# Building the attention's search mask on TensorE: scores made a second time, the masked gap added to them, and the engines' slots redone

## The reference, cut to what matters

```python
scores = jnp.einsum('bthd,bghd->bhtg', Q, K) / np.sqrt(DH)
scores = jnp.where(vision_mask[:, None, None, :], scores, -jnp.inf)
topv, topi = jax.lax.top_k(scores, K_TOP)          # K_TOP = 32
probs = jax.nn.softmax(topv, axis=-1)
attn = jnp.zeros_like(scores).at[bi, hi, ti, topi].set(probs)
attn_mean = attn.mean(axis=1)                      # over the 4 heads
c_t = jnp.einsum('btg,bgd->btd', attn_mean, V)
```

## Time and profile before

| | us |
|---|---|
| three runs, median (lowest, highest) | 1743.46 (1742.68, 1745.92) |
| the profiled execution's own time | 1737.76 |
| its span, first to last instruction | 1735.6 |
| mean granted TensorE clock in it | 0.959 |

### The profile page before, as it was taken

One profiled execution on the slowest core, in us unless ns is written; L12 is line 12 of the kernel. 1 busy time (PEld: TensorE's weight loads), 2 busy tenths in 40 slices (PEclk: granted clock), 3 DMA queues, 4 the chain that ended last, 5 costly groups with the idle time before them and its releaser, 6 DMA issues.

```text
span 1735.6 us, 22438 instructions
## 1 busy us (share of the span) xinstructions
PE 1535.6 (88%) x7358; PEld 1135.2 (65%) x7369; DVE 1350.4 (78%) x2168; ACT 1146.9 (66%) x2101; POOL 1195.9 (69%) x1341
## 2 busy tenths in 40 slices
PE   4878868898889898889998999899989998999996
PEld 2456546665656565667686767676767776767896
DVE  5798799988998898978888888888888995111321
ACT  2388875686678658765887588757876687134442
POOL 1388775858876786788678876897689858633422
PEclk9899889998998999899999999999999999999999
DMA  7210031002200210123322331333132211842431
GB/s 199 54 34 4 20 104 31 13 19 61 43 13 25 64 35 13 36 74 95 95 73 62 76 94 51 76 82 98 46 80 65 86 32 40 266 143 88 95 50 22
DMA packets 97223, 115.27 MB, mean 66 GB/s; under 512 B 17840, under 2 KB 74168, under 8 KB 96964
## 3 DMA queue, kind: packets, MB, share of 16 engines
q1 hardware_dynamic: 85348, 100.32, 19.9%
q0 software_dynamic: 11760, 13.52, 5.2%
HBM read 75.48 MB, written 19.58 MB: 55 GB/s over the span
## 4 chain that ended last, share of the span: by engine, by line
PE 31%; DVE 28%; POOL 16%; ACT 16%; issue 7%; DMA 2%; SPq 1%; POOLq 0%; DVEq 0%
DVE R L1460 9%; DVE ZB L1464 7%; POOL ZB L773 4%; PE PS L2191 4%; DVE ZB L1456 4%; ACT ZB L1049 3%; PE PS L2039 3%; PE PS L1770 3%; PE PS L2068 2%; DVE R L1452 2%; ACT R L1052 2%; ACT R L1055 2%; PE PS L1820 2%; POOL ZB L775 2%; PE PS L2027 2%
## 5 line engine op out<-in xcount | busy, mean ns | idle before, releaser
L1460 DVE MAX8 R<-ZB 128x8 f32<-128x1024 f32 x384 | 471.1, 1227 | 10.9
L1770 PE MATMUL PS<-R 128*128 128x256 f32 x1118 | 290.4, 394 | 26.0 <-ACT R L1052 14.6
L1464 DVE MATCH_REPLACE8 ZB<-R,ZB 128x1024 f32<-128x1024 f32 x256 | 309.5, 1209 | 0.0
L773 POOL TENSOR_TENSOR ZB<-ZB 128x1024 f32<-128x1024 f32 x96 | 231.7, 2414 | 68.4 <-ACT ZB L1049 68.2
L1052 ACT ACTIVATE R<-PS 128x512 f32<-128x512 f32 (+6 forms) x404 | 173.3, 467 | 143.2 <-PE PS L2039 47.3
L1770 PEld LDWEIGHTS PS<-R 128*128 128x128 f32 x1118 | 211.2, 198 | 72.7 <-ACT R L1052 24.2
L775 POOL TENSOR_TENSOR ZB<-ZB 128x1024 f32<-128x1024 f32 x96 | 226.6, 2360 | 7.5
L1452 DVE MAX8 R<-PS 128x8 f32<-128x1024 f32 x128 | 155.9, 1218 | 6.9 <-PE PS L1793 6.9
L1456 DVE MATCH_REPLACE8 ZB<-R,PS 128x1024 f32<-128x1024 f32 x128 | 155.5, 1215 | 0.0
L1049 ACT ACTIVATE ZB<-ZB,R 128x1024 f32<-128x1024 f32 x128 | 147.1, 1149 | 4.2
L1049 ACT ACTIVATE ZB<-PS,R 128x1024 f32<-128x1024 f32 x128 | 141.6, 1106 | 3.1 <-DVE R L1472 2.8
(11 more groups left out here) (256 smaller groups left out, 3150.1 us busy)
## 6 DMA issues: line engine op xcount, KB each, us to landing
ZR<-ZR SPq DMA_DIRECT2D x96, 128.0 KB
ZB<-in_L_ffn_rt_gate SPq DMA_DIRECT2D x21, 512.0 KB
ZB<-in_L_ffn_rt_up SPq DMA_DIRECT2D x21, 512.0 KB
ZB<-in_L_ffn_rt_down SPq DMA_DIRECT2D x21, 512.0 KB, 5.9
R<-in_x SPq DMA_DIRECT2D x16, 512.0 KB, 3.9
ZB<-in_ctx SPq DMA_DIRECT2D x8, 768.0 KB, 4.8
R<-xs_d SPq DMA_DIRECT2D x39, 128.5 KB, 2.1
out<-R SPq DMA_DIRECT2D x32, 128.0 KB, 3.7
```

What stands on the lines that cost most here:

```text
L773: pool.tensor_tensor(e, e, w, ALU.mult).then_inc(s.g_att, 1)
L1460: vec.max(ml[:, 8 * r:8 * r + 8], w).then_inc(s_tk[n % 2], 1)
L1464: vec.match_replace(w, ml[:, 8 * r:8 * r + 8], w, NEG).then_inc(s_tk[n % 2], 1)
L1770: pe.matmul(q_bank(*key)[:, 0:256], ident, warm, start=True, stop=True)
```

## The change

The mask no longer is an array that POOL multiplies with. Once the 32nd largest is known, ACT writes the gap as bf16 into `gap[n % 2]` (the first half of tk's words). PE then makes the scores a second time into the same banks and adds, by one more bf16 matmul per bank with a diagonal `steep` of -2^66, the gap times -2^66 (`cuts`, four matmuls a unit). ACT takes one exponential of the result, with -max*SCALE - log(sum) as its bias, so that e comes out masked and divided by the sum. POOL only adds: three additions for four heads (head 0 and 1 in one), none for the first. The second DVE operation of `limits` becomes a tensor_scalar with two operations in place of the reciprocal.

The waits follow: the scores of n+2 now wait for the exponential of n (a_att), which waits for the cut of n (p_cut), which waits for the gap (a_gap). The first replacement of n+2 waits for the cut of n instead of POOL's product. Transfers that refill qt and kt wait for the cuts.

`warm` is now R[:, 0:256], and keep_warm waits for the constants instead of tri. The loads of gout and bout share a semaphore with gin, bin and b2. All slot tables are new. The FILL tables sum to 413 matmuls over the kernel where they summed to 559.

```diff
-        warm = R[:, alloc.top:alloc.top + 256]
+        warm = R[:, 0:256]
...
+        gap = [w[:, 0:512].bitcast(BF16) for w in tk]
         ee = [alloc_b(1024), alloc_b(1024)]
+        steep = alloc_b(64).bitcast(BF16)
...
@@ sync
-                        on.wait_ge(s.p_sc, 16 * (b - 1) + 8)
+                        on.wait_ge(s.p_cut, 16 * (b - 1) + 8)
...
@@ gpsimd attention
-                    on.wait_ge(s.a_att, 5 * n + 5)
-                    if h == 0:
+                    on.wait_ge(s.a_att, n + 1)
+                    if h == 1:
                         if t:
                             on.wait_ge(*q_run("finish", t - 1, 1))
-                        pool.tensor_tensor(acc, e, w, ALU.mult).then_inc(s.g_att, 1)
+                        pool.tensor_tensor(acc, ee[0], ee[1], ALU.add).then_inc(s.g_att, 1)
                     else:
-                        pool.tensor_tensor(e, e, w, ALU.mult).then_inc(s.g_att, 1)
-                        on.wait_ge(s.g_att, 7 * t + 2 * h)
-                        pool.tensor_tensor(acc, acc, e, ALU.add).then_inc(s.g_att, 1)
+                        on.wait_ge(s.g_att, 3 * t + h - 1)
+                        pool.tensor_tensor(acc, acc, ee[n % 2], ALU.add).then_inc(s.g_att, 1)
...
@@ scalar
+            def limits():
+                for n in range(16 * B):
+                    ml, q = mx[n % 3], sm[n % 3]
+                    yield tile_at(n) + ACT_GAP[n % 16]
+                    on.wait_ge(s_tk[n % 2], PASS * (n // 2) + 7)
+                    act.activation(gap[n % 2], sc_bank(n), ACT.Relu, bias=ml[:, 31:32], scale=-1.0).then_inc(s.a_gap, 1)
+                    yield tile_at(n) + ACT_SUM[n % 16]
+                    on.wait_ge(s.v_limit, 2 * n + 1)
+                    exp(junk, ml, ACT.Exp, bias=q[:, 0:1], scale=SCALE, accum_out=q[:, 1:2]).then_inc(s.a_gap, 1)
+                    on.wait_ge(s.a_gap, 3 * n + 2)
+                    exp(q[:, 2:3], q[:, 1:2], ACT.Ln).then_inc(s.a_gap, 1)
+
             def attention():
                 for n in range(16 * B):
                     yield tile_at(n) + ACT_EXP[n % 16]
+                    on.wait_ge(s.p_cut, n + 1)
+                    on.wait_ge(s.v_limit, 2 * n + 2)
                     on.wait_ge(s.g_att, added(n - 2))
-                    exp(e, sc_bank(n), ACT.Exp, bias=q[:, 0:1], scale=SCALE).then_inc(s.a_att, 1)
...
-                    exp(w, w, ACT.Exp, bias=q[:, 3:4], scale=-STEEP).then_inc(s.a_att, 1)
+                    exp(ee[n % 2], sc_bank(n), ACT.Exp, bias=sm[n % 3][:, 3:4], scale=SCALE).then_inc(s.a_att, 1)
...
@@ vector
+                TS(steep, ident, -STEEP, None, ALU.mult).then_inc(s.v_ones, 1)
...
-                    on.wait_ge(s.g_att, taken(n - 2))
+                    on.wait_ge(s.p_cut, n - 1)
                     vec.match_replace(w, ml[:, 0:8], sc_bank(n), NEG).then_inc(s_tk[n % 2], 1)
...
-                    on.wait_ge(s.a_att, 5 * n + 2)
-                    vec.reciprocal(q[:, 2:3], q[:, 1:2]).then_inc(s.v_limit, 1)
+                    on.wait_ge(s.a_gap, 3 * n + 3)
+                    on.wait_ge(s.a_att, n - 2)
+                    TS(q[:, 3:4], ml[:, 0:1], -SCALE, q[:, 2:3], ALU.mult, ALU.subtract).then_inc(s.v_limit, 1)
...
@@ tensor
-                    on.wait_ge(s.ld_tri, 16)
+                    on.wait_ge(s.ld_cst, 16)
...
-                    on.wait_ge(s.a_att, 5 * (n - 2) + 3)
+                    on.wait_ge(s.a_att, n - 1)
...
+            def cuts():
+                for n in range(16 * B):
+                    b, i, h = n // 16, n // 4 % 4, n % 4
+                    yield tile_at(n) + PE_CUT[n % 16]
+                    keep_warm(FILL_CUT[n % 16], next_bank(tile_at(n) + PE_CUT[n % 16], -1))
+                    on.wait_ge(s.v_ones, 4)
+                    on.wait_ge(s.a_gap, 3 * n + 1)
+                    o = (2 * b + i // 2) % 3 * 256 + 128 * (i % 2)
+                    for lo in (0, 512):
+                        pe.matmul(sc_bank(n)[:, lo:lo + 512], qt[0:97, h, o:o + 128], kt[0:97, h, lo:lo + 512], start=True, stop=False)
+                        ins = pe.matmul(sc_bank(n)[:, lo:lo + 512], steep, gap[n % 2][:, lo:lo + 512], start=False, stop=True)
+                    ins.then_inc(s.p_cut, 1)
...
-FILL_PREP = (0, 1, 0, 0, 0, 0, 3, 0, 0)
+FILL_PREP = (0,) * 9
```

More of the change, by code:

```diff
@@ new lines @@
+ACT_SILU = ((-165.3, 132.2), (131.6, -23.6))
+ACT_SH = ((138.7, 10.6, 46.4, -355.7), (145.5, 64.5, -336.9, -426.8))
+DVE_SPECTRUM = ((151.1, -137.8, 115.5, 142.5), (54.5, -176.7, 33.2, -626.3))
+DVE_MOMENTS = ((159.8, 173.7), (-320, 98.2))
+DVE_ROUTE = ((174.2, 176.4), (127.3, -215.8))
+ACT_PREP = (5.4, 15.2, -988.5)
+ACT_QUERY = (27.3, -30.2, 27.6)
+ACT_CONTEXT = (0.9, 57.5)
+ACT_KEY = (11.2, 62.2)
+ACT_FINISH = ((-1, -33.2, 5.1, 17.2), (13.4, 9.7, 18.7, 27.5), (17.8, -50.2, 20.9, 24.5), (-1.4, -9.2, 4.6, 7.1))
@@ L483, in queried @@
             return 192 * sum(2 if 2 * k % 3 == 2 else 1 for k in range(b + 1))
-        def taken(n):
-            return 7 * (n // 4) + (1, 2, 4, 6)[n % 4] if n >= 0 else 0
         def added(n):
-            return 7 * (n // 4) + (1, 3, 5, 7)[n % 4] if n >= 0 else 0
+            return 3 * (n // 4) + (1, 1, 2, 3)[n % 4] if n >= 0 else 0
         def row2(x, n):
@@ L1405, in routed @@
                     act.activation(acts[j % 3], PS[:, 1, :], ACT.Silu).then_inc(s.a_silu, 1)
-            weave(attention(), finish(), prep(), keys(), weights(), kernel_rows(), kernel_values(), post(), shared(), tiles(), routed())
+            weave(limits(), attention(), finish(), prep(), keys(), weights(), kernel_rows(), kernel_values(), post(), shared(), tiles(), routed())
         @block.vector
@@ L1817, in finish @@
                     on.wait_ge(*q_free("finish", t, 2))
-                    on.wait_ge(s.v_ones, 4 if b else 3)
+                    on.wait_ge(s.v_ones, 5 if b else 3)
                     for g in range(8):
@@ L2205, in routed @@
                 yield LAST_AT - 14.5
[L2206 removed]
+                on.wait_ge(s.a_att, 16 * B)
                 on.wait_ge(s.v_run, B)
@@ L2218, in routed @@
                         down(k - 2)
-            weave(setup(), attention(), finish(), prep(), weights(), kernel_rows(), kernel_values(), post(), ranks(), shared(), tiles(), routed())
+            weave(setup(), attention(), cuts(), finish(), prep(), weights(), kernel_rows(), kernel_values(), post(), ranks(), shared(), tiles(), routed())
 _INS = ['x', 'ctx_768', 'mask_BxS_bf1', 'mask_BxS2_bf1', 'g_xattn', 'g_ffn', 'L0_xattn_Wq', 'L0_xattn_Wk', 'L0_xattn_Wv',
```

235 lines of the change are left out of this document (108 added, 127 removed), and 21 rows, old and new, of tables (DVE_TOP, POST_AT).

## The result

The changed kernel takes **1753.7 us** (median of 6 runs, 1751.2 to 1755.3) against 1743.1 us before (6 runs on the same chip, 1735.6 to 1745.9): ratio 1.0061, 95% interval 1.0040 to 1.0081. It is 0.6% slower; the forecast was 1709, faster, with 1754 inside its range. Its profiled execution spans 1752.1 us.

What follows compares the result with a forecast made beforehand. The kernel was taken as bound by a loop through four engines, DVE heaviest, PE close beside in late frames. Terms -23.5 - 27 + 19 - 6 = -37.5, with 3.5 taken back: -34 from 1743.5 gives 1709 us, range 1668 to 1760.

Steps and rivals of the forecast that it cites:

- Pool and the single tails: Multiplications gone from POOL and shorter tails of single units on the chain: -23.5 and -27 us.
- The bank: Scores of n+2 wait for n's gap, cut and exponential: 0 us, losing as much as before; as a rival 0.08.
- the one behind the scatters: Late frames and behind the last unit: POOL leaves the scatters with two additions left, 4.7 us less, five times: -23.5 us.
- single units' tails: Where the chain runs through one unit's tail: 4.1 us instead of 5.1, -27 us, between +8 and -57.
- PE: Cuts add 115 us on PE against fewer fills; +19 us in all, from 0 to 32.
- TensorE's measure: Judging PE by matmul starts; by LDWEIGHTS' busy share 30% of a late frame is free, the sum 19 us lower.
- PE has room: Rival: cuts fall only where PE idled, so the +19 goes: 1690 us, chance 0.10.
- The setup: Fill ahead of L1843 no longer waits 8.8 us for tri: -6 us, between -9 and 0.
- DVE's small operation: On DVE, 1 us later behind a gap, often behind the next unit's first pass: 3.5 us taken back.
- The waits that were to decide: Forecast wrong where DVE's first max waiting for scores, or PE for the gap before the cut, takes back over 34 us.
- PE as the bound: Rival: late frames 3.4 us longer each, early gains vanish: 1747 us, 1761 with cuts at 1.1 us; chance 0.17.
- The clock: Rival: with fewer fills TensorE's clock falls to 0.88, +4 us each early frame: 1721 us, chance 0.04.

Runs made afterwards that it cites:

- b_load: Kernel before with the change's setup part, plus four more 97x512 matmuls on TensorE ahead of each unit's scores, overwritten by them: 1771.9 us, ratio 1.0177.
- b_nomul: Kernel before with the setup part, without the mask's multiplications on Pool, which only copies and adds: 1714.0 us, ratio 0.9825.
- a_nolog: Changed kernel, DVE's second small operation without subtracting the logarithm and without its wait for ScalarE's sum and logarithm: ratio 1.0044 to the kernel before.
- a_load: Changed kernel with the scores of each cut made once more (two more 97x512 matmuls, overwritten): ratio 1.0274 to the kernel before.
- b_setup: Kernel before with the change's setup part alone (warm operand, wait for the constants, no fills in prep): 1730.3 us, ratio 0.9930.
- a_nofill: Changed kernel with none of its 413 fill matmuls: ratio 1.0254 to the kernel before.
- b_load_hold: Kernel before with setup part, no Pool multiplications, b_load's added matmuls, and scores waiting for ScalarE's last operation two units before in 12 of 16 units: ratio 1.0181.
- b_load_fill: b_load with each place's fills cut to four fifths, 433 instead of 527 matmuls: ratio 1.0108 to the kernel before.
- a_clock: Changed kernel with six fills ahead of the second key product of the preparation in three early frames: ratio 1.0061 to the kernel before.

## Why the prediction was wrong

The runs give a sum that can be laid beside mine: setup -12, Pool's relief -17 (mean of -18 and -16), TensorE's load +44 (43 and 45), fewer fills -12, the bank's hold +17; together +20 against a measured +11. The 9 us between lie within the errors of five differences. That the sum closes so well is partly luck: by halves of the search it does not (see what stays open), and the terms were measured in the old order. The -12 for the fills is b_load's; in the changed kernel itself a fifth fewer gave nothing.

Of the 45 us between forecast and result, 33 lie in Pool's relief, 17 in the bank and 13 in PE, and the setup gives 6 back.

- **Pool and the single tails, -50: the step that failed.** I read 66 us of L773 on the chain and 63 us of DVE's waits as time to be had, and under "The bank" I wrote in the same breath that the new path would lose as much as the old one's 63 us. It does: 77.4 us of waits before, 84.5 after. But these are the same microseconds, and they can't be won in one line and given back at 0 in another. The relief by itself is 17 us. Of the two parts, the one behind the scatters, -23.5, had the right place: in the profile of b_nomul the gain lies in the late frames, at 3 to 4 us each. The first quarter of such a frame falls by 2 us there (41.9 from 43.7), so the fall to 37.6 us in the changed kernel is mostly not the relief's. Of the 27 us of single units' tails nothing is seen. That term's range also has a slip: 4.8 against 5.1 us on 27 pieces is a gain of 8 us at the least, not a loss of 8.
- **PE, +19 within 0 to 32.** Measured +44 - 12 = +32. The cut's length was right (843.34 to 844.28 us in the chain, 0.94), and so was the number of fills. Mis-sized is the share that shows: I counted the cuts that fall into the unbroken piece of the old chain, 15 us and 4 net of fills, a sixth of the 115. Net it is 32, more than a quarter; the load alone shows with 43 of 118, more than a third. My reading of it, argued and not separated by a run, is that PE's queue is in fixed order and everything behind a cut is later, whether the old chain passed there or not.
- **TensorE's measure.** I followed matmul starts and not the share of the weight loads. The piece of the chain around the cut above decides it: from 843.4 to 850.3 us PE's matmuls follow each other without a gap, at full clock, while the loads fill 3.61 of 6.90 us:

```profile
843.40:850.30 6.90, 6.90 (x21) 3.61 (x21) 3.97 (x5) 2.81 (x4) 3.79 (x6) 1.00 0.00 0
```

The Trainium skill (Perfetto Trace Analysis, Identifying the Most-Contended Engine) would judge TensorE's headroom by MFU (the arithmetic done, as a share of the peak) and the busy share of LDWEIGHTS. By the latter nearly half of this piece was free, and 30% of the late frame; the trace disagrees. The rival "PE has room" falls by b_load's 43 us.
- **The bank, 0 within -63 to +64.** Measured +17, by a hold that is longer by logarithm and mask alone, in 12 of 16 units.
- **The setup, -6 within -9 to 0.** Measured -12 (-17 to -8), 9.0 of it seen at the first search. DVE's first wait ended at 12.35 us, not 16: with no fills in prep, nothing stood ahead of L1781.
- **DVE's small operation, +3.5.** Its wait grew to 44.3 us, and a_nolog puts its worth at 3, which can't be told from nothing. The size fits, though the row looked ten times as large.
- **Busy times** came as forecast: POOL 896.6 (890), ACT 1026.6 (1000, which is 27 too low), PE 1590.4 (1590). The frames did not: early 170.9 against 160 to 163, late 176 to 181 (from unit 64, 80 and 96) against 170 to 175. The waits that were to decide, first max for scores and PE for the gap, are 40.2 and 31.5 us.
- **The rivals.** PE as the bound had the right kind and nearly the time (1747, or 1761 with long cuts) but the wrong place: its late frames don't grow, the early ones lose 6.6 to 6.8 us each. I had called the early frame roomy for its 19 us of idle. For the old order that holds in part: b_load adds 13 us before unit 64 and 30 behind, and with Pool relieved all of the load's cost lies behind. In the new order it does not: a_load adds 15 us before unit 64 and 16 behind. The clock: 0.964 against 0.959, so it played no part in the total, though it moved between the runs of the sum (0.949 in b_setup, 0.963 in b_load), and each of their terms is net of that. That it can cost is shown by a_nofill, with 0.900 and less, and 34 us. There the Trainium skill's rule on throttling after idle gaps (TensorE: Matmul & The Clock Gate, HAM oscillation) agrees with the trace: without the fills PE is busy for 83% of the span instead of 91%.

**What stays open.** Relief and load alone leave the first 64 units at 678.1 us, the hold brings them to 691.3, the changed kernel has 705.4; from unit 64 on it is the other way, 720.5, 725.2 and 693.2. So the changed kernel is 14 us worse early and 32 better late than b_load_hold, and these two, each larger than the 11 us to be explained, cancel in the sum. Fewer fills took 6 us off either half in b_load_fill, so they don't explain the two. What is left belongs to the slots (theory S) and the new waits together, and no run here separates them. That the place of the clock's fall is the cause early is excluded by a_clock.

## What to carry to other kernels

A wait that the profile names is not a gain until you have said what is late next: one of 69 us here was worth 18, one of 44 about 3. In a kernel whose queues are in fixed order, don't price an engine's added work only by what the old chain passes through. The share that shows was 43 of 118 us in the old order, 37 of 60 on the cut in the new, and 2 of 40 for fills taken away. So measure it at the place in question; one run that doubles existing matmuls there does so before anything is built. And look at what a change carries along: of this one the setup's three lines, alone, are the better kernel, 0.9930 of the time before.

## What was not expected of the hardware

The row of the cut's bf16 weight loads, L1810, looks like a cost that it is not. 241 of 256 loads have an idle of 0.25 us each ahead of them, 60.2 us in all:

```profile
L1810 PEld LDWEIGHTS PS<-ZB 128*128 128x128 bf16 x256 | 25.4, 99 | 62.4 <-issue 60.2
```

But that is idle of the weight loads alone. In the chain the four matmuls of a cut follow each other in 0.24, 0.23, 0.24 and 0.23 us, with nothing between them, and waits of this kind also stand ahead of fp32 loads (185 of them at L2086, 44.4 us).

With six fills in the idle stretch ahead, the granted clock behind the gate was 1.00 instead of 0.57 in the second early frame (2.4 GHz throughout) and still 0.58 in the first, by the windows of a_clock. And a multiplication on POOL whose second operand is one repeated column takes 1.93 to 2.03 us where two full operands take 2.40.
